# A graph layer and a mixture of experts on one core: the routing tail spread over three tiles, low weight parts cut by VectorE

## What is computed

```python
n1 = layernorm(x)
deg = max((adj != 0).sum(-1), 1)
pooled = (adj + I) @ n1 / deg + n1        # deg of the row's own node
x1 = x + relu(pooled @ W + b)
xf = layernorm(x1)
top2 of softmax(xf @ Wr + br), their weights scaled to a sum of 1
y = sum over the 2 experts: weight * (gelu(xf @ W1[e] + b1[e]) @ W2[e] + b2[e])
out = x1 + xf + y            # 16 experts, 256 -> 512 -> 256
```

## Time and profile before

| | |
|---|---|
| median of 3 runs | 850.42 us (849.53 to 852.34) |
| the profiled execution | 847.92 us |
| its span, first to last instruction | 846.2 us |
| busy: TensorE, VectorE, ScalarE, POOL | 639.4, 561.1, 369.9, 316.3 us |
| mean granted TensorE clock | 0.904 |
| DRAM traffic | 103.71 MB read, 25.83 MB written |

### The profile page before, as it was taken

One profiled execution on the slowest core, in us unless ns is written; L12 is line 12 of the kernel. 1 busy time (PEld: TensorE's weight loads), 2 busy tenths in 40 slices (PEclk: granted clock), 3 DMA queues, 4 the chain that ended last, 5 costly groups with the idle time before them and its releaser, 6 DMA issues.

```text
span 846.2 us, 17877 instructions
## 1 busy us (share of the span) xinstructions
PE 639.4 (76%) x4701; PEld 478.1 (56%) x4702; DVE 561.1 (66%) x1763; ACT 369.9 (44%) x583; POOL 316.3 (37%) x277
## 2 busy tenths in 40 slices
PE   0188678777878686878787723978878899999995
PEld 0166556665656565656566611655555577667773
DVE  4977767776877777777787861555655655555563
ACT  2775455646554554555456411334333333333331
POOL 2722333334333423242334346143333344444444
PEclk9999879897888888897989957799999999999998
DMA  9677574757665665757575522455455544443430
GB/s 291 194 203 232 146 238 147 213 167 205 200 195 185 189 216 152 228 174 227 147 233 157 210 78 63 119 109 117 121 113 113 115 79 71 72 71 64 72 64 1
DMA packets 65917, 126.78 MB, mean 150 GB/s; under 512 B 9547, under 2 KB 40559, under 8 KB 65360
## 3 DMA queue, kind: packets, MB, share of 16 engines
q1 hardware_dynamic: 40240, 72.27, 28.6%
q10 hardware_dynamic: 10368, 35.66, 14.2%
q0 software_dynamic: 15264, 18.31, 12.1%
HBM read 103.71 MB, written 25.83 MB: 153 GB/s over the span
## 4 chain that ended last, share of the span: by engine, by line
PE 30%; DVE 22%; DMA 13%; issue 12%; ACT 11%; ACTq 4%; POOL 3%; SPq 1%; DVEq 1%; POOLq 1%
DMA out_dram<-orows,at_xg 8%; PE bank L507 6%; PE bank L530 6%; PE bank L458 4%; PE bank L460 4%; DVE at_xg L774 4%; ACT a L572 4%; DVE pooled L833 4%; ACTq L240 3%; DMA wst<-in_L_ffn_W_dram 3%; PE bank L431 2%; PE bank L515 2%; ACT orows L612 2%; ACT feat L599 2%; PE bank L407 2%
## 5 line engine op out<-in xcount | busy, mean ns | idle before, releaser
L458 PE MATMUL bank<-wall,at_xg 128*128 128x257 f16 x1024 | 281.0, 306 | 40.9 <-DMA brb<-in_L_ffn_br_dram 30.6
L460 PE MATMUL bank<-wall,at_xg 128*128 128x256 f16 x1024 | 274.9, 304 | 0.0
L1224 POOL DMA_INDIRECT out_dram<-orows,at_xg x79 | 124.0, 1570 | 191.7 <-DMA out_dram<-orows,at_xg 111.0
L572 ACT ACTIVATE a<-abuf 128x1024 f16<-128x1024 f32 x128 | 134.6, 1052 | 122.2 <-DVE at_xg L774 117.7
L458 PEld LDWEIGHTS bank<-wall,at_xg 128*128 128x128 f16 x1024 | 115.6, 113 | 65.1 <-issue 42.1
L507 PE MATMUL bank<-wall,feat 128*128 x474 | 119.6, 390 | 27.4 <-DVE feat L1039 17.8
L703 ACT ACTIVATE a<-a 128x512 f32<-128x512 f32 x79 | 49.8, 630 | 180.1 <-DVE a L1048 180.1
L460 PEld LDWEIGHTS bank<-wall,at_xg 128*128 128x128 f16 x1024 | 111.7, 109 | 23.6
L1054 DVE SCALAR_TENSOR_TENSOR wg<-bank,xseT 128x512 f16<-128x512 f32 x79 | 54.6, 691 | 92.2 <-ACT xseT L709 92.2
L530 PE MATMUL bank<-wall,xseT 128*128 x632 | 110.1, 276 | 0.0
L1190 POOL DMA_INDIRECT rows<-feat,posi x64 | 64.3, 1004 | 89.2 <-DVE posi L919 79.4
(11 more groups left out here) (150 smaller groups left out, 969.7 us busy)
## 6 DMA issues: line engine op xcount, KB each, us to landing
abuf<-in_adj_dram SPq DMA_DIRECT2D x64, 512.0 KB, 8.8
abuf<-in_adj_dram ACTq DMA_DIRECT2D x64, 512.0 KB, 9.1
wst<-in_L_ffn_W_dram SPq DMA_DIRECT2D x32, 512.0 KB, 7.0
at_xg<-rows SPq DMA_DIRECT2D x79, 136.0 KB, 2.2
out_dram<-orows SPq DMA_DIRECT2D x32, 128.0 KB
abuf<-in_L_ffn_b_dram SPq DMA_DIRECT2D x4, 1024.0 KB, 10.4
wall<-in_x_dram ACTq DMA_DIRECT2D x8, 256.0 KB, 13.4
wall<-in_x_dram SPq DMA_DIRECT2D x8, 256.0 KB, 13.3
```

The lines of the kernel that those rows point to most:

```text
L458: both = [lambda: pe.matmul(ps_acc[odd][:, 0:D + 1], w, xh[:, j, 0:D + 1], start=j == 0, stop=j == T - 1), lambda: pe.matmul(ps_acc[odd][: ...
L460: lambda: pe.matmul(ps_acc[odd][:, 0:D], w, xl[:, j, :], start=False, stop=False)]
L572: act.activation(a16[:, c % 2, :].rearrange("p (a w) -> p a w", a=Q), arrived[:, k % 2, :, c * w:(c + 1) * w], ACT.Copy).then_inc(ev("cast ...
L1224: L.indirect_dma_start(out, bass.IndirectOffsetOnAxis(ap=info[r][:, 0:1].bitcast(U32), axis=0), orow[r], None, bounds_check=N - 1, oob_is_ ...
```

## The change

The tail takes three rounds instead of two (DEPTH = 3). In round t, tile s = t-1 goes from pool_x to x1's statistics, tile r = t-2 from rstd1 to top2, tile v = t-3 from rank to list_tokens. ScalarE's casts run three chunks ahead instead of four. x1, the transposed xf (xfT) and two bases have their own places in orows; the transposed xf has its own PSUM bank (ps_X), and the counts are kept in PSUM (ps_P) by TensorE. The own row of each node (the I above) is added by two products with the identity (own_rows), the bias by a product with gb_ones; relu is ScalarE's. The base is xf scaled by ScalarE plus x1 added by POOL. The top 2 are taken of the logits, and only one exponential is needed. cut_low_weights moves from POOL to VectorE as one pass, and ScalarE's second scaling goes. In the expert stage late weights are loaded two cuts (four blocks) ahead.

```diff
-CAST = 4
+CAST = 3
+DEPTH = 3
...
-    x1 = pooled
+    x1 = orows[:, 0, :]
+    xfT = orows[:, 1, :]
-    base = orows[:, 7, :]
+    base = [orows[:, 7 - k, :] for k in range(2)]
```

SP's step, and its start of the expert stage:

```diff
-                sp.wait_ge(ev("cast"), t * CH)
+                sp.wait_ge(ev("cast"), t * CH + CH)
                 for b in QUEUE[0]:
-                    load_adj(sp, i, k + 1, b)
+                    load_adj(sp, i, k + 2, b)
...
-            if late(q, r) is not None:
-                load_late(late(q, r))
+            if late(q, r) is not None and late(q, r) + 2 < 2 * (E - EARLY):
+                load_late(late(q, r) + 2)
...
+        load_late(0)
+        load_late(1)
         for r in range(AHEAD):
             load_block(0, r)
```

TensorE's step, and the waits ahead of its first product:

```diff
+                if g == 0 and has_t:
+                    own_rows(t, odd)
+                if g == 1 and has_v:
+                    rank(v, 1 - odd)
+                if g == 2 and has_s:
+                    pooled_T(s)
+                if g == 3 and has_r:
+                    xf_T(r)
+                if g == 5 and has_s:
+                    graph_out(s)
+                if g == 5 and has_v:
+                    count(v, 1 - odd)
+                if g == 6 and has_r:
                     logits(r)
-                if g == 1 and has_s:
-                    pooled_T(s)
-                if g == 7 and has_s:
-                    xf_T(s)
-                if g == GRAPH - 1 and has_s:
-                    graph_out(s)
-                if g == (7 if last else 4) and has_r:
-                    rank(r)
...
         pe.wait_ge(ev("consts_in"), 16 * len(consts))
+        after(pe, "gb_cut", 0)
+        after(pe, "wg_cut", 0)
+        after(pe, "gb_ones", 0)
```

ScalarE's step:

```diff
-                if g == 0 and has_r:
-                    copy_xf_T(r)
-                if g == 2 and has_s:
-                    high_pooled_T(s)
...
+                if g == 1 and has_v:
+                    exps(v)
+                if g == 1 and is_(t, lambda t: 1 <= t < T - 2):
+                    more_adj(i, k + 2)
+                if g == 3 and has_s:
+                    high_pooled_T(s)
+                if g == 2 and has_r:
+                    high_part(i, k - 2)
+                    scale_base(i, k - 2)
+                if g == 4 and has_r:
+                    copy_xf_T(r)
...
+                if g == 6 and has_s:
+                    relu(s)
+                if g == 7 and is_(t, lambda t: t < T):
                     normalize_x(t)
-                if g == 7 and has_s:
-                    high_part(i, k - 1)
-                    make_base(s)
```

VectorE's pool_x, and the moved cut:

```diff
-            V.tensor_tensor(pooled[:, :], ps_acc[odd][:, 0:D], xs, ALU.add).then_inc(ev("acc_read"), 1)
-            after(V, "acc_read", s)
+                after(V, "pooled_T", s - 1)
             after(V, "dinv", s)
-            V.scalar_tensor_tensor(out=pooled[:, :], in0=pooled[:, :], scalar=deg[:, 1:2], in1=xs,
+            V.scalar_tensor_tensor(out=pooled[:, :], in0=ps_acc[odd][:, 0:D], scalar=deg[:, 1:2], in1=xs,
                                    op0=ALU.mult, op1=ALU.add).then_inc(ev("pooled"), 1)
...
+            V.scalar_tensor_tensor(out=wall[:, bass.ds(w_at(i, which, 1), n)], in0=wst[:, which, :], scalar=SW,
+                                   in1=wall[:, bass.ds(w_at(i, which, 0), n)],
+                                   op0=ALU.mult, op1=ALU.subtract).then_inc(ev("w_cut"), 1)
```

POOL's step:

```diff
+            if is_(r, lambda r: 0 <= r < T):
+                rstd1(r)
+                low_part(r, odd)
+                make_base(i, k - 2)
+            if is_(v, lambda v: 0 <= v < T):
+                list_tokens(v, 1 - odd)
```

More of the change, by code:

```diff
@@ L214, in passed @@
         eng.sem_inc(ev("passed"), 1)
-    CONSTANTS = 12
+    CONSTANTS = 13
+    base_out = [sem(f"base_out{k}") for k in range(2)]
     x_in = [sem(f"x_in{c}") for c in range(XC)]
@@ L272, in over_tiles @@
                 step(i, k)
-        for k in range(RUN + 2):
+        for k in range(RUN + DEPTH):
             step(T // RUN - 1, k)
@@ L411, in graph_out @@
             after(pe, "pooled_T_low", s)
+            if is_(s, lambda s: s >= 1):
+                after(pe, "relued", s - 1)
+            pe.matmul(ps_Z[:, 0:D], gb_ones[:, :], gbm[:, :], start=True, stop=False)
             n = 0
@@ L440, in step, with own_rows @@
+        def own_rows(t, odd):
+            for part in (xh[:, bass.ds(t, 1), 0:D], xl[:, bass.ds(t, 1), :]):
+                pe.matmul(ps_acc[odd][:, 0:D], id16[:, :], part.rearrange("p n d -> p (n d)"), start=False, stop=False)
         def step(i, k):
             t, odd = tile(i, k), k % 2
-            s, r = t - 1, t - 2
+            s, r, v = t - 1, t - 2, t - 3
             has_t = is_(t, lambda t: t < T)
@@ L445, in step @@
             has_r = is_(r, lambda r: 0 <= r < T)
-            last = isinstance(t, int) and t == T
+            has_v = is_(v, lambda v: 0 <= v < T)
             for g in range(G):
@@ L801, in _ @@
                                op0=ALU.mult, op1=ALU.subtract).then_inc(ev("wg_cut"), 1)
+        after(V, "gb_high", 0)
+        V.scalar_tensor_tensor(out=gbm[P // 2:P, :], in0=gb[P // 2:P, :], scalar=SG, in1=gbm[P // 2:P, :],
+                               op0=ALU.mult, op1=ALU.subtract).then_inc(ev("gb_cut"), 1)
         after(V, "b2_high", 0)
@@ L870, in top2 @@
-        def top2(s):
-            after(V, "exps_made", s)
-            V.reciprocal(sc[:, 2:3], sc[:, 1:2]).then_inc(ev("sum_inv"), 1)
-            after(V, "sum_inv", s)
-            V.tensor_scalar(pr[:, :], ex[:, :], sc[:, 2:3], None, ALU.mult).then_inc(ev("probs"), 1)
-            after(V, "probs", s)
+        def top2(i, k):
+            r, odd = tile(i, k), k % 2
+            after(V, "logits", r)
+            V.scalar_tensor_tensor(out=lg[:, :], in0=ps_S[:, 0:E], scalar=1.0 / SX, in1=brb[:, :],
+                                   op0=ALU.mult, op1=ALU.add).then_inc(ev("lg_made"), 1)
+            after(V, "lg_made", r)
+            if is_(r, lambda r: r >= 1):
+                after(V, "exps_made", r - 1)
@@ L1032, in _ @@
         V.wait_ge(ev("b1_in"), 16 * CH)
-        V.wait_ge(ev("base_out"), 16 * T)
+        for k in range(2):
+            V.wait_ge(base_out[k], 16 * T // 2)
         def copy_tokens_T(q, r):
@@ L1174, in rstd1, with make_base @@
             L.tensor_tensor(vr[:, 1:2], vr[:, 0:1], mhalf[:, 0:1], ALU.pow).then_inc(ev("x1_rstd"), 1)
+        def make_base(i, k):
+            after(L, "base_scaled", tile(i, k))
+            L.tensor_tensor(base[k % 2], base[k % 2], x1, ALU.add).then_inc(ev("base_made"), 1)
         def low_part(s, odd):
```

290 lines of the change are left out of this document (139 added, 151 removed).

## The result

| | before | after |
|---|---|---|
| median | 849.97 us (848.67 to 852.34, 4 runs) | **750.54 us** (748.18 to 751.4, 4 runs) |
| ratio to before | | 0.8823, 95% interval 0.8794 to 0.8852 |
| span of the profiled execution | 846.2 us | 746.5 us |
| mean granted TensorE clock | 0.904 | 0.951 |

The forecast was 748 us, with 710 to 800 as range (the rivals' times in it are reckoned from 749). The spans differ by 99.7 us, and the timeline says where. I cut both traces at the reciprocal of the degree in pool_x, which follows a tile's products at once, and at weigh.

What follows compares the result with a forecast made beforehand. No engine was full, so waits at the graph stage's round edges bound the kernel; VectorE with POOL beside it would be next. 847.9 − 84.9 + 5.8 − 3 − 19 = 746.8, with the median's offset 748 us; range 710 to 800.

Steps and rivals of the forecast that it cites:

- The old waits go: Graph-stage round edge: base, xf_T and logits come a round later in own buffers, ending TensorE's 2 us wait for xf_T's copy.
- clock 1.00: Sign of a right prediction: TensorE's clock is full from 60 us to the end of the graph stage.
- Rival 3: Graph stage, every round: TensorE stays at half clock, 18.6 us a round, about 978 us in total; chance 0.03.
- a wait of over 1 us a round that it does not name: Sign against the prediction: such an unnamed wait, or a loop clock under 0.95, makes it wrong.
- The round: Graph stage: 11.2 us instead of 13.94, VectorE busy or held by POOL 10.6; over 31 rounds −84.9 us.
- The DMA term: Graph-stage transfers: share 0.62 × 13.94 = 8.7 us a round, with nothing added by the change.
- Rival 1: Graph stage: high_part waits for lists of two tiles before; round 4.1 + L, 12.8 us at L 8.7; 799 us; chance 0.25.
- Rival 2: Graph stage: VectorE's small operations miss POOL's, round about 10.3 us, 28 us less, 721 us; chance 0.2.
- The moved cut: Early weights' cut, POOL to VectorE: 1.225 us every second round, 0.61 a round; the skill's contention rule would add 0.6.
- The start: Before the first product: TensorE waits for wg_cut and gb_cut, tile 0 ends at 57.6 instead of 51.8, +5.8 us.
- The drain: From the last tile's products to the first pads: 16.4 instead of 20.8, less later weight loads, so −3 us.
- The experts: Blocks 0 to 31: earlier late-weight loads give 3.89 instead of 4.44 us a block, 17.1, plus 4.3 before; −19 us.

## Why the prediction was right, and where not

**The time was right, 748 for 750.5, and most of its terms; the reason that I gave for the largest one was not, and that its size came out is luck.**

- *The old waits go.* Right. No wait of TensorE for the copy of the transposed features is among the listed ones, and the clock went from 0.904 to 0.951. In the loop half clock is left in single stretches, as at 275.50 above, so "clock 1.00" was too much: 0.96 from 100 to 350 us. Rival 3 is out. But the prediction also said what would make it wrong, a wait of over 1 us a round that it does not name, and there is one: the casts' wait for the adjacency, 50.4 us in the 24 rounds from 100 to 380 us, 2.1 a round.
- *The round, 11.2 us forecast, 11.26 measured.* The size was right, its cause wrong. I added 1.2 us for small operations of VectorE that POOL holds, and said that VectorE would be busy or held 10.6 us. It was busy 67%, some 7.7 us a round; even its own work was priced too high, at 9.4, as was ScalarE's, 7.8 without its DMA issues for 6.9. Held operations do exist, but only where the two meet. The CAST of put_places took 0.17 us in 30 of its 32 instances, and was held in the two that fell beside L1206:

```profile
78.62 1.16 POOL L1206 TENSOR_TENSOR feat<-xf,feat 128x512 f16<-128x512 f32 x1 [3.36 <-ACT feat L635]
```
```profile
78.83 0.98 DVE L938 CAST posi<-posf 128x2 int32<-128x2 f32 x1
...
400.55 0.98 DVE L938 CAST posi<-posf 128x2 int32<-128x2 f32 x1
```

  In 29 of 32 tiles L1206 runs beside low_pooled_T (L866, from PSUM), which takes 0.42 there, as elsewhere.
- *The DMA term, 8.7 us a round.* **This is the step that failed.** I took share times period, 0.62 × 13.94, as what the transfers need. That supposes that busy DMA engines move as much as before, 191 / 0.62 = 308 GB/s. In a stage with transfers in flight all the time they moved 240, and the 2.77 MB of a round take 11.5 us. The two mistakes, 1.2 us for held operations plus the allowance for coupling, and some 2.8 us too little for the transfers, happened to meet: weights left out gave 10.0 us a round with all of VectorE's work in it.
- *Rival 1, the ring of the lists.* **Its mechanism came, at another price.** The sign that I had named for it, high_part waiting for the lists in most rounds, is there: 28.9 us of waiting in 20 of 24 rounds, and 23% of the longest chain are the lists' landing, against 4% for the adjacency's. Its sum was 4.1 + L, with L the landing of the second list, 12.8 for the 8.7 us that I took. The median over all lists is 6.5 us from 100 to 350 us, but over the second ones it is 7.5, and 4.1 + 7.5 = 11.6 is the measured round. When weights were left out or moved, L and the round fell together. So the ring and the full DMA engines give the same 11.5, and no run separates them: none opened this ring and closed no other. What is shown is that the round hangs on the transfers, and that VectorE does not hold it.
- *Rival 2, everything overlaps, 10.3.* Its condition held, operations of VectorE missed POOL's. The bytes kept the round from it.
- *The moved cut.* Forecast 1.225 each; the 16 cuts from 63.1 to 402.3 us took at most 1.226. Beside 15 of them POOL issued lists (L1219), which did not lengthen them; none had a TENSOR_TENSOR of POOL beside it. By the rule of the Trainium skill (GPSIMD Engine Reference, 1. Specifications) on contention with POOL the round would have been up to 0.6 longer, if the cut had met low_part; it met it in none of the 16. What I did not see is that POOL's relief was worth 10 us.
- *The start.* +5.9 for +5.8, with the mechanism as told.
- *The drain.* **Wrong in sign.** I had the tail 4.3 us shorter, 3 after the delay of SP's loads. The first pads come at 428.70, 23.1 us after tile 31's last product (405.6), where before it was 20.8. The ring of the lists is closed here too, and no products are left beside it:

```profile
411.96 0.63 ACT L635 ACTIVATE feat<-xf 128x512 f16<-128x512 f32 x1 [5.91 <-DMA rows<-feat,posi]
...
419.92 0.63 ACT L635 ACTIVATE feat<-xf 128x512 f16<-128x512 f32 x1 [1.80 <-DMA rows<-feat,posi]
```

  I had one wait for a list, landed 8.5 us after the last product; there are two, one after the other, the first until 411.96, 6.4 after it, and the second with its low_part and base until 422.5. The price is the third tile of the tail, which I had not followed.
- *The experts.* −18.8 in blocks 0 to 31 where 17.1 were forecast, 3.84 us a block for 3.89. Ahead of block 0 the late loads gave 5 us (4.3 forecast), most of which the drain took. Both together: 21.5 for 22.

## What to carry to other kernels

A DMA share below 1 is not spare capacity in the same proportion: before counting on it, count the bytes of a round and ask what rate this mix reaches when something is always in flight. When a change closes idle time, the transfers are the first thing to price anew. A round that alternates with the presence of one transfer says that its bytes count, but not by which way. A ring is priced with the landing that it waits for, here the second list's and not the average of both, and it can be closed in every round though the waits that show it are short. An order of work on one engine that waits for two sides (POOL's lists and base) is worth trying both ways, since opening one ring can close another.

## What the runs showed that I had not expected

- The same loads ran at about 400 GB/s in the second half of a burst (408 at 254 us before) and at 240 on average where the queues never ran empty, with the share at 1.0 in both; within that stage short stretches had 186 and 328, as above. So a share of 1.0 names no rate. It follows neither the quarter, nor, but for a few GB/s, the partition half, nor the rows that are read. What it does follow I can't say from these runs: the burst's first half is as slow although the queues were empty ahead of it. It stays open.
- The order of quarters that puts both queues on one partition half first cost 14 us against its mirror, and 20 against the order in use, at nearly the same average rate in the loop (233, 237, 240 GB/s). 6.5 of the 14 and 11.1 of the 20 were lost before tile 0's degree.
- Loading late weights ahead was worth 27 us in the kernel before by its medians, and 24.5 by its traces, more than the whole of the waits for them (18.5 us); 4.9 of it came ahead of block 0, where the first cut stood ahead of VectorE's work.
